# Two graph layers on one core: index tables on chip, a product kept in PSUM, and three chunks in the second layer's messages

## The reference

```python
h = jnp.maximum(_layernorm(x, axis=-1), 0.0)
x = x + _L0_gnn_ref(h, node_vec1, edge_attr_4, edge_attr_8, ..., src, dst, 16)
h = jnp.maximum(_layernorm(x, axis=-1), 0.0)
x = x + _L1_gnn_ref(h, edge_attr_4, W1, W2, W3, W4, W5, Ws, Wv, edge_index)
# in layer 0, per edge (gs, gv: rows of lin1(h) at the source; w1_..w4_: a small network of edge_attr_8)
m0a = gs * ys * w1_
m0b = jnp.sum(gv * yv[:, None, :], -1) * INV3 * w4_
m1a = gs[..., None] * yv[:, None, :] * w2_[..., None]
m1b = gv * ys[..., None] * w3_[..., None]
mid = jax.ops.segment_sum(edge_feat, edge_dst, num_segments=N)
jnp.cos(angle) * scfeat + jnp.sin(angle) * conv
# in layer 1, per edge (ss, vv: the source row; e0, e1: the edge's scalar and vector)
dot = jnp.einsum('eui,ei->eu', vv, e1)
out0 = C0 * (ss * e0 @ W1 + dot * INV3 @ W2)
p3 = (ss @ W3)[:, :, None] * e1[:, None, :] * INV3
p4 = jnp.einsum('eui,uw->ewi', vv * e0[:, :, None], W4) * INV3
p5 = jnp.einsum('eui,uw->ewi', jnp.cross(vv, e1[:, None, :]), W5) * INV6
m_agg = jax.ops.segment_sum(m, dst, num_segments=n)
x + jax.nn.relu(m_agg @ (Ws, Wv))
```

## Time and profile before

| what | us |
|---|---|
| median of 3 runs | 2458.61 |
| the profiled execution | 2459.89 |
| its span | 2458.1 |
| VectorE busy | 1873.4 (76%) |
| PE busy | 1824.8 (74%) |
| POOL busy | 1477.5 (60%) |
| granted TensorE clock, mean | 0.883 of full |

### The profile page before, as it was taken

One profiled execution on the slowest core, in us unless ns is written; L12 is line 12 of the kernel. 1 busy time (PEld: TensorE's weight loads), 2 busy tenths in 40 slices (PEclk: granted clock), 3 DMA queues, 4 the chain that ended last, 5 costly groups with the idle time before them and its releaser, 6 DMA issues.

```text
span 2458.1 us, 51427 instructions
## 1 busy us (share of the span) xinstructions
PE 1824.8 (74%) x12730; PEld 1696.7 (69%) x12730; DVE 1873.4 (76%) x5982; ACT 1296.0 (53%) x3409; POOL 1477.5 (60%) x1432
## 2 busy tenths in 40 slices
PE   0788888888888888888888554544543788898887
PEld 0287778777787777877777544444443788888887
DVE  2099999999999999999999676666666566665564
ACT  0256666666666666666666555555555333333332
POOL 1045455554545555455553677777777777777776
PEclk9999999999999999999999755555555899998999
DMA  9445555555555555555555534334433334444443
GB/s 85 145 139 186 196 206 202 196 188 195 200 201 203 190 195 191 201 205 194 195 184 185 172 108 118 114 116 123 117 117 117 94 105 111 115 111 110 113 115 85
DMA packets 236558, 377.35 MB, mean 154 GB/s; under 512 B 116353, under 2 KB 146108, under 8 KB 236364
## 3 DMA queue, kind: packets, MB, share of 16 engines
q1 hardware_dynamic: 189484, 302.66, 39.1%
q0 software_dynamic: 47040, 74.31, 11.2%
HBM read 183.27 MB, written 201.21 MB: 156 GB/s over the span
## 4 chain that ended last, share of the span: by engine, by line
PE 33%; issue 17%; DVE 14%; ACT 12%; DMA 12%; POOL 6%; SPq 4%; ACTq 1%; DVEq 1%; POOLq 0%
ACT h L774 6%; PE bank L981 5%; DMA q_row<-row_tab 4%; PE bank L976 4%; DMA x_all<-in_xa,i_dst 3%; DVE st L1207 3%; POOL h_all L612 3%; PE bank L1090 3%; PE bank L982 3%; PE bank L1066 2%; DMA out<-yo,i_put 2%; POOL x_all L606 2%; PE bank L1158 2%; ACT h L889 2%; ACT tot L832 2%
## 5 line engine op out<-in xcount | busy, mean ns | idle before, releaser
L649 POOL TENSOR_TENSOR yo<-x,h 128x640 f32<-128x640 f32 x196 | 303.9, 1551 | 506.2 <-ACT h L774 504.9
L981 PE MATMUL bank<-wp,hT 128*128 128x160 f32 x1568 | 376.3, 322 | 0.0
L774 ACT ACTIVATE h<-x,nmr,inv 128x160 f32<-128x160 f32 x784 | 342.2, 514 | 1.5 <-DVE nmr L1211 1.5
L606 POOL DMA_INDIRECT x_e<-in_xa,i_src x192 | 210.8, 1098 | 161.1 <-issue 78.3
L981 PE MATMUL bank<-wp,eT 128*128 128x160 f32 x784 | 263.0, 428 | 51.2 <-ACT eR L897 43.7
L982 PE MATMUL bank<-wp,hR 128*128 128x64 f32 x1568 | 259.4, 247 | 0.0
L1358 DVE SCALAR_TENSOR_TENSOR x<-bank,scl,x_all 128x160 f32<-128x160 f32 x784 | 254.7, 365 | 5.1 <-PE bank L982 1.8
L982 PEld LDWEIGHTS bank<-wp,hR 128*128 128x128 f32 x1568 | 255.5, 190 | 0.0
L612 POOL DMA_INDIRECT out<-yo,i_put x196 | 209.7, 1070 | 74.3 <-issue 41.0
L612 POOL DMA_INDIRECT h_all<-h,i_put x196 | 217.4, 1109 | 59.8 <-issue 58.9
L976 PE MATMUL bank<-ident,h_e 128*128 128x128 f32 x392 | 83.9, 353 | 215.8 <-DVE hr_e L1527 215.4
(11 more groups left out here) (161 smaller groups left out, 5508.3 us busy)
## 6 DMA issues: line engine op xcount, KB each, us to landing
x_all<-in_xa SPq DMA_DIRECT2D x98, 644.0 KB, 5.0
h_all<-h SPq DMA_DIRECT2D x98, 640.0 KB, 3.0
out<-yo SPq DMA_DIRECT2D x98, 640.0 KB, 3.3
q_row<-row_tab SPq DMA_DIRECT2D x98, 256.0 KB
sum_tab<-tot SPq DMA_DIRECT2D x49, 322.0 KB, 4.2
y_tab<-yo SPq DMA_DIRECT2D x49, 320.0 KB
x<-y_tab SPq DMA_DIRECT2D x49, 320.0 KB
cv<-sum_tab SPq DMA_DIRECT2D x25, 322.0 KB, 3.2
```

The source lines that it names most:

```text
L606: nc.gpsimd.indirect_dma_start(into[:, t * width:(t + 1) * width], None, rows, bass.IndirectOffsetOnAxis(ap=index[:, t:t + 1], axis=0)).th ...
L649: nc.gpsimd.tensor_tensor(yo[j][:, a:b], x1[j][:, a:b], h1[j][:, a:b], ALU.add).then_inc(d_y, 1)
L774: ins = nc.scalar.activation(h1[j][:, k * D:(k + 1) * D], x1[j][:, k * D:(k + 1) * D], ACT.Relu, bias=nmr2[j][:, k:k + 1], scale=inv2[j][: ...
L981: nc.tensor.matmul(dst_ps, main[:, t * P:(t + 1) * P], wp[:, w:w + D], start=True, stop=False)
```

## The change

1. *Tables.* The stores to `src_tab`, `dst_tab`, `put_tab`, `key_tab` and from `t_row` go. The tables stay in SBUF; `row_tab` is filled by one copy from a new input `dst_rows` (destinations, one row per tile). VectorE copies a quad's indices into `i_src`, `i_dst`, `i_put` (128x4). The key of `same` is read from `f_dst`.
2. *Carry.* `carry` is zero but for its last row, which VectorE computes once for all tiles in setup and a DMA of 2 KB per quad brings in; the comparison goes.
3. *Edge network.* Four loads ahead instead of two.
4. *First pass.* The inverse goes to PSUM, and inverse and scale stand ahead of the first two x1 of a step's second half. The first vector feature part becomes two instructions, one of which writes to PSUM, from where the third part reads.
5. *Second layer's messages.* ScalarE scales the row by e0; VectorE forms the products into `prod`, and then dot and cross from them, behind the message of n-2. Features take three chunks instead of four, the parts four products instead of five (`msg1d` goes, and five of 16 weight products of the setup). The row table is loaded a quad ahead, in its own step; the scatter index no longer waits on SP.

```diff
-            sp.dma_start(src_tab.rearrange("q p c -> p q c"), t_src[:, :].rearrange("p (q c) -> p q c", c=GQ)).then_inc(s_tab_out, 16)
...
-            sp.dma_start(row_tab[0:TA, :], t_row[0][0:TA, :]).then_inc(s_tab_out, 16)
+            load_rows(dst_rows, s_row_in)
...
+            sp.dma_start(row_tab, dst_rows).then_inc(s_rows, 16)
...
-                wait(sp, n_mm, 2 * (g - 1))
+                wait(sp, n_mm, 2 * (g - 3))
...
+            def p1_carry(q):
+                j = q.mod(2)
+                wait(sp, e_seg, q.times(GQ, -GQ))
+                sp.dma_start(carry[j][P - 1:P, :], carry_q[q.times(1)].unsqueeze(0)).then_inc(e_ca[j], 16)
...
-                wait(sp, m_put[j], q.over(2, 64))
-                sp.dma_start(i_put[j][:, :], put_tab[q.times(1)]).then_inc(m_px[j], 16)
...
+            def p3_step(q, ahead=True):
+                if ahead:
+                    p3_rows(q + 1)
+                p3_edges(q)
+                p3_y(q)
+                p3_carry(q)
...
             def dense_inverse(u):
-                j = u.mod(4)
                 v.wait_ge(d_sq1, u.times(1, 1))
-                V.reciprocal(inv1[j][:, :], sd1[j][:, :]).then_inc(d_scl, 1)
+                V.reciprocal(bank[2][:, 2 * D:2 * D + GD], sd1[u.mod(4)][:, :]).then_inc(d_inv, 1)
...
-                selector(same, q.mod(2), 0)
-                selector(carry, q.mod(2), 1).then_inc(e_sc, 1)
+                selector(q).then_inc(e_sc, 1)
...
+            def index_copy(into, table, q, signal):
+                V.tensor_copy(into[:, :], table[:, bass.ds(q.times(GQ), GQ)]).then_inc(signal, 1)
...
-                    V.tensor_tensor(f[:, 128:320].rearrange("p (a u i) -> p a u i", a=2, i=3),
-                                    w[:, 128:192].rearrange("p (a u) -> p a u", a=2).unsqueeze(3).to_broadcast([P, 2, DU, 3]),
-                                    g[:, DS:D].rearrange("p (u i) -> p u i", i=3).unsqueeze(1).to_broadcast([P, 2, DU, 3]),
-                                    ALU.mult).then_inc(e_fm, 1)
+                    V.tensor_tensor(turned, bc_last(w[:, 160:192], 3), vec, ALU.mult).then_inc(e_fm, 1)
+                    V.tensor_tensor(f[:, 128:224].rearrange("p (u i) -> p u i", i=3), bc_last(w[:, 128:160], 3), vec, ALU.mult)
...
-                    V.tensor_tensor(f[:, 224:320].rearrange("p (u i) -> p u i", i=3),
-                                    f[:, 224:320].rearrange("p (u i) -> p u i", i=3),
+                    V.tensor_tensor(f[:, 224:320].rearrange("p (u i) -> p u i", i=3), turned,
                                     bc_mid(ed(j, t, 1, 4), DU), ALU.mult).then_inc(e_ft, 1)
...
+            def p3_dot_cross(n):
+
+                v.wait_ge(m_pr, n.times(1, 1))
                 wait(v, m_ftr, n.times(1, -1))
...
+                V.tensor_reduce(f[:, D:D + DU], dot, AX.X, ALU.add)
+                V.tensor_tensor(cross[:, :, 0:2], a[:, :, 0:2], b[:, :, 1:3], ALU.subtract)
+                V.tensor_tensor(cross[:, :, 2:3], a[:, :, 2:3], b[:, :, 0:1], ALU.subtract).then_inc(m_ft, 1)
...
             def p3_slot(n):
                 if n.within(T):
                     p3_features(n)
                 if (n - 2).within(T):
                     p3_message(n - 2)
+                if n.within(T):
+                    p3_dot_cross(n)
                 if (n - 4).within(T):
                     p3_out(n - 4)
...
-                nc.scalar.activation(feat[n.mod(2)][:, 448:512], h1[j][:, t * D:t * D + DS], ACT.Copy).then_inc(m_ss, 1)
+                f, h = feat[n.mod(2)], h1[j][:, t * D:(t + 1) * D]
+                nc.scalar.activation(f[:, 0:D], h, ACT.Copy, scale=ed(j, t, 0, 1))
+                nc.scalar.activation(f[:, 288:352], h[:, 0:DS], ACT.Copy).then_inc(m_ss, 1)
```

More of the change, by code:

```diff
@@ L207, in gnn_kernel @@
         feat = two("feat", [P, 512])
[L208 removed]
+        fT = two("fT", [P, 384])
+        prod = two("prod", [P, 3 * DV])
         xr = two("xr", [P, CW])
@@ L1624, in p2_step @@
                     p2_stats(q)
+                if (q + 3).within(Q):
+                    index_copy(i_dst[(q + 3).mod(4)], t_gat, q + 3, r_ix)
+                if c:
+                    wait(v, r_put[q.mod(2)], (q - 2).over(2, 64, -64))
+                    index_copy(i_put[(q - 2).mod(4)], t_put, q - 2, r_px)
                 if b:
@@ L1659, in p2_step @@
                     p2_angle(q, 7)
+            for q in range(3):
+                index_copy(i_dst[q], t_gat, At(0, q), r_ix)
             v.wait_ge(d_y, 2 * U)
@@ L1731, in p3_slot @@
                     p3_same(n + 1)
-                if n.mod(4) == 0 and n.within(T):
-                    selector(carry, n.c // GQ % 2, 1).then_inc(m_sc, 1)
+            for q in range(2):
+                index_copy(i_src[q], t_src, At(0, q, 2), m_ix)
             p3_same(At(0, 0, 8))
```

386 lines of the change are left out of this document (194 added, 192 removed).

## The result

The changed kernel takes 2463.44 us, the median of 15 runs (2459.88 to 2464.99); the kernel before takes 2456.44 beside it (15 runs). The ratio is 1.0032 [1.0021, 1.0043]: the change costs some 8 us. The forecast was 2443, a gain of 16 us.

A forecast was written before the change was run, and what follows sets the result against it. Bounds: SP's queue in setup, the circuit through PE, ScalarE, POOL and VectorE in the first pass, POOL afterwards, then a new loop in the last stage. Terms -44 + 6 + 0 + 22 = -16 gave 2443 us; range 2390 to 2510.

The forecast's parts named there:

- Setup: Setup and edge network: table stores leave SP's queue and loads run four ahead; -44 us, bounds -34 to -50.
- First pass: First pass: small additions in the circuit, 49 quads at 0.13 us each; +6 us, bounds 0 to +10.
- (a): First pass, inverse and scale: scale no longer held, but the centring still starts only at 710.4; 0.
- (c): First pass: index copy of 128x4 between statistics and outer part, in the circuit; about 0.08 us.
- (b): First pass: one feature instruction of 192 elements becomes two of 96; some 0.05 us more, once a quad.
- the circuit: First pass: PE, ScalarE, POOL's add, VectorE from centring to feature, PE; VectorE's slowness outside it costs nothing.
- the step that said 0: Node update: index copies on idle VectorE, POOL issues as before; 0, bounds -20 to +15 us for phase.
- the loop: Second layer's messages: PE's work and VectorE's piece follow each other in every tile; 2.81 us a tile, +21 us.
- 195 x 2.81: Second layer's messages: 195 tiles at 2.81 us make 548 against 527; +21 us, bounds -20 to +48.
- Rival 3: Second layer's messages: PE's clock drops, such tiles take about 4.55 us; 35 of them give 2504 us; chance 0.28.
- Rival 1: Last stage: POOL rules at 2.6 us a tile, not the loop; total about 2400 us; chance 0.12.
- rival 2: First pass: PE's wait of 41 us comes back, quad of 24.7 us; total about 2396 us; chance 0.10.

The follow-up runs named there:

- e10: Changed kernel with the edge network's loads two groups ahead instead of four; 2469.23 us.
- e7: Changed kernel with the first pass's index copy moved from between statistics and outer part to behind the same step's features; 2461.50 us.
- e6: Changed kernel with the first pass's vector features as before the change: one instruction of 192 elements into SBUF; 2457.46 us.
- e2: Changed kernel with the first pass's dense centring moved behind the features of the step's second tile; 2428.34 us.
- e3: Changed kernel with three tiny VectorE memsets (128x4) added ahead of the node update's centring; 2447.76 us.
- e1: Changed kernel with dot and cross of tile n placed ahead of the message of tile n-2; 2414.32 us.
- e4: Changed kernel with 44 unused PE transposes of the identity added ahead of the last stage; 2457.07 us.
- e11: Changed kernel with one wait of dot and cross (transposes of n-2 done) moved to the head of the features of n; 2458.70 us.
- e5: Changed kernel with both VectorE waits for dot and cross moved ahead of the message of n-2, arithmetic order kept; 2474.32 us.
- after: The changed kernel itself, without any follow-up edit; 2463.44 us.
- e9: Changed kernel with two of the old table stores put back on SP's queue ahead of the network's first load; 2493.08 us.

## Why the prediction was right or wrong

The time lies in the range; the sign was wrong. Of the 21 us between forecast and profile (-16 against +5), the last stage has 17, the node update 8.5, and the setup gave back 3. Each stage lies inside its own bounds, and so does the tile of the last stage (2.902 in 2.7 to 2.95): the sign hung on the middles of the last two terms, and these failed.

- **Setup: right, in part by luck.** -47.2 for -44. PE's start came at 23.77 (24 to 25 forecast), and the deeper loads were worth 5.6 by e10 for 4.5. One of the new row loads held the queue for 6.57 us (at 5.03), where some 0.4 were put down, and the scalars went out at 13.59 instead of about 11; but their copy had landed by 21.77, and from SP's issue to PE it took 2.0 instead of 3.0.
- **First pass: right, with its parts.** +5.2 for +6. The centring took over the hold (a), the index copy costs 0.07 a quad by e7 (c), the split parts 0.06 by e6 (b); 0.13 a quad is what was forecast. The third part's hold went as the Trainium skill says (SBUF — State Buffer, Who interferes with whom: a VectorE instruction with at most one SBUF input does not contend with GpSimd); 244 ns for 564 agree. But 320 ns off 196 instructions were worth nothing, since the hold went over to the next instruction with two inputs in SBUF, `same` (e6), and PE waits for the circuit (e2).
- **Node update: the step that said 0 failed,** at +8.5, inside its bounds of -20 to +15. The mechanism in the bounds was the right one: phase against POOL's DMAs, whose time above 0.98 grew by 8.5. What moved the phase was not what the prediction named. The copies put the centring 0.15 later, as it said; but the gathered rows come 0.44 sooner, and so the centring stands ahead of POOL's DMA in 41 of 45 quads instead of about 10. That the landing would change was not in the prediction; why it did stays open. "0" was the middle of an unknown phase, and e3 shows that three tiny instructions decide between +8.5 and -2. What the Trainium skill infers in the same section, that a tensor_tensor does not touch descriptor generation, does not hold for these rows: 0.98 becomes 1.50 to 1.58.
- **Last stage: the loop was right, its size was not.** This is the step that turned the sign: the term 195 x 2.81, which took the undisturbed tile for every tile. An undisturbed tile does take 2.82, and e1 opens the loop with one move. But the mean is 2.902; 0.09 x 195 = 18 us were missing. About 8 are the start at the lower level (e4): the sum took every tile at the full level. Some 2 to 5 are a wait of dot and cross, which the sum counted at nothing (e11, and e5 from the other side). The rest, 5 to 8, lies for the most part in two of a loop turn's eight tiles (2.895 and 3.019 in e11); what the engines do there was not tried, and it stays open.
- **Rival 3** had the right place at the wrong size: the lower level was there in the first five tiles and not in 35; three of them take 4.59, where 4.55 was worked out. **Rival 1** (2.6 a tile) and **rival 2** (a quad of 24.7) did not come by this change, but each is about what one move gives: 2.634 in e1, 24.84 in e2. The price of the loop against POOL's floor, 52 us, and of the circuit, 36, are what the change left lying.

## What to carry to other kernels

When work is put behind an instruction that waits for another engine, walk the dependences round once: if that engine in turn needs the work, the two alternate, and a stage that no engine fills takes the sum of both; put the work ahead of the wait. An instruction made faster pays only if some other engine waits for it, and a hold that is removed from it is taken over by the next instruction that can be held. Where the price of a small addition is its phase against another engine's DMAs, give the bounds and no middle, and try a shift of a fraction of a microsecond.

## What the runs showed of the hardware

- A VectorE instruction with two inputs in SBUF (128x512, 0.68 us) that starts 0.04 to 0.2 us ahead of a GpSimd indirect DMA makes it 1.37 to 1.73 us instead of 0.98 (1.55 to 1.71 in after, 1.37 to 1.51 in e3). One that starts more than 0.05 us behind the DMA's start leaves it at 0.98 to 1.01. Closer to that start both occur (0.98, and 1.73 to 1.80).
- Where several waits stand ahead of one VectorE instruction, the blocking one can become an instruction of its own, and the start behind it comes 0.10 us later: xr at 0.14 instead of 0.04 behind PE's end (e5).
- Behind 26 us without work PE is at the lower level (granted clock 0.50) for its first five tiles, 21.8 us in after, with 0.75 us without work in each of the three that take 4.59, and then at the full one. With 7.2 us of transposes without a gap just ahead, the tiles start at the full level (e4).
- Two stores of 128x49 pieces of four indices behind each other delay the loads behind them longer than they hold the queue themselves: 8.8 us of their own, 13.6 us more in the loads' issue (e9).
